# Attention gate: x's high and low parts through one product of four 256-column matmuls, halves added on VectorE

## What is computed

```
q, k, v = x @ Wq, x @ Wk, x @ Wv        # q, k: silu, then a rotation ("rope")
o       = chunked linear attention over q, k, v, with a running state per head
gate    = x @ Wg1 @ Wg2                 # Wg1: 512 x 32, Wg2: 32 x 512
o       = o * sigmoid(gate)
o       = o / sqrt(mean over each head of o*o + eps) * norm_weight
x1      = x + o @ Wo
out     = x1 + down( gelu(n(x1) @ gate_W) * (n(x1) @ up_W) )     # n: layer norm
```

## Time and profile before

| | |
|---|---|
| median of three runs | 1288.82 us (1288.71 to 1288.97) |
| the profiled execution | 1288.75 us, its span 1286.7 us |
| busy share of the span | TensorE 99%, VectorE 71%, ScalarE 37%, GpSimd 34% |
| granted TensorE clock | full speed in every slice of the span |
| attention and passage | the first 300 us or so of the span; `gate1` runs 16 times in them |

### The profile page before, as it was taken

One profiled execution on the slowest core, in us unless ns is written; L12 is line 12 of the kernel. 1 busy time (PEld: TensorE's weight loads), 2 busy tenths in 40 slices (PEclk: granted clock), 3 DMA queues, 4 the chain that ended last, 5 costly groups with the idle time before them and its releaser, 6 DMA issues.

```text
span 1286.7 us, 20699 instructions
## 1 busy us (share of the span) xinstructions
PE 1270.3 (99%) x7376; PEld 1043.5 (81%) x7376; DVE 917.0 (71%) x1594; ACT 475.2 (37%) x799; POOL 435.2 (34%) x360
## 2 busy tenths in 40 slices
PE   9999999998999999999999999999999999999998
PEld 6888888887788888888888888888888888888887
DVE  7878788788867667676767676767767666767665
ACT  5433434434433333333333433333333333333421
POOL 2434455564442322223132324133232324232400
PEclk9999999999999999999999999999999999999999
DMA  9000000000001000010000000001001000000003
GB/s 326 12 2 1 19 17 2 2 1 2 25 25 33 17 33 27 22 33 28 29 24 24 24 24 24 33 16 33 24 24 33 24 33 24 24 24 24 24 13 119
DMA packets 21778, 40.23 MB, mean 31 GB/s; under 512 B 2660, under 2 KB 2916, under 8 KB 21604
## 3 DMA queue, kind: packets, MB, share of 16 engines
q1 hardware_dynamic: 21060, 39.47, 9.4%
q10 hardware_dynamic: 672, 0.13, 0.1%
HBM read 35.40 MB, written 4.19 MB: 31 GB/s over the span
## 4 chain that ended last, share of the span: by engine, by line
PE 93%; DVE 2%; POOL 1%; ACT 1%; issue 1%; POOLq 0%; DVEq 0%; ACTq 0%
PE bank L1351 16%; PE bank L1354 15%; PE bank L1353 15%; PE bank L1197 13%; PE bank L1199 13%; PE bank L1198 13%; PE bank L1211 2%; PE bank L1291 1%; PE bank L1310 1%; PE bank L1300 1%; PE bank L1343 1%; PE bank L1331 1%; PE bank L1258 0%; ACT xg L394 0%; PE bank L1257 0%
## 5 line engine op out<-in xcount | busy, mean ns | idle before, releaser
L883 DVE TENSOR_TENSOR acc<-acc,bank 128x512 f32<-128x512 f32 x248 | 169.3, 683 | 129.4 <-PE bank L1199 129.3
L1197 PE MATMUL bank<-wdh,hh 128*128 128x512 f32 x512 | 199.3, 389 | 0.0
L1199 PE MATMUL bank<-wdh,hl 128*128 128x512 f32 x512 | 199.2, 389 | 0.0
L1198 PE MATMUL bank<-wdl,hh 128*128 128x512 f32 x512 | 199.2, 389 | 0.0
L1351 PE MATMUL bank<-xoh,wgh 128*128 128x512 f32 x448 | 175.9, 393 | 0.6 <-DVE cxa L891 0.6
L1351 PE MATMUL bank<-xoh,wuh 128*128 128x512 f32 x448 | 175.1, 391 | 0.7 <-ACT cxa L482 0.7
L1354 PE MATMUL bank<-xoh,wgl 128*128 128x512 f32 x448 | 174.5, 390 | 0.0
L1354 PE MATMUL bank<-xoh,wul 128*128 128x512 f32 x448 | 174.3, 389 | 0.0
L1353 PE MATMUL bank<-xol,wuh 128*128 128x512 f32 x448 | 174.3, 389 | 0.0
L1353 PE MATMUL bank<-xol,wgh 128*128 128x512 f32 x448 | 174.3, 389 | 0.0
L899 DVE TENSOR_TENSOR hl<-hx,hh 128x512 fp32r<-128x512 f32 x128 | 113.5, 887 | 51.4 <-ACT hh L489 51.0
(11 more groups left out here) (163 smaller groups left out, 2285.7 us busy)
## 6 DMA issues: line engine op xcount, KB each, us to landing
stg<-packed_dram SPq DMA_DIRECT2D x48, 256.0 KB, 2.5
stg<-scales_dram SPq DMA_DIRECT2D x48, 256.0 KB
out_dram<-acc SPq DMA_DIRECT2D x16, 256.0 KB, 2.0
acc<-x_dram SPq DMA_DIRECT2D x3, 1024.0 KB, 15.0
w_in<-wq_dram SPq DMA_DIRECT2D x2, 512.0 KB, 5.2
w_in<-wk_dram SPq DMA_DIRECT2D x2, 512.0 KB, 6.9
w_in<-wv_dram SPq DMA_DIRECT2D x2, 512.0 KB, 8.6
w_in<-wo_dram SPq DMA_DIRECT2D x2, 512.0 KB, 11.2
```

The source lines that it names most:

```text
L883: V.tensor_tensor(row, row, BY[j % 2][:], ALU.add).then_inc(y_add, 1)
L1197: pe.matmul(dst, w_h, x_h, start=start, stop=False)
L1198: pe.matmul(dst, w_h, x_l, start=False, stop=False)
L1199: return pe.matmul(dst, w_l, x_h, start=False, stop=stop)
```

## The change

`gate1` issues one matmul for each of the four channel blocks, over 256 columns: 128 of x's high part and 128 of its low part, side by side, into 256 columns of `BS[3]`. For that the high and low parts of x (and of the output, which tile 1's x borrows) lie in one tile each, `xt` and `ot`; the names `xth`, `xtl`, `oth`, `otl` stay as views of them. The two halves have then to be added. ScalarE copies the first to a new SBUF tile `gs` (`gate_copy`), VectorE adds the second from PSUM into `gs` (`sum_gate`), and the old steps `gate_low` on both engines read `gs` instead of the bank. Two semaphores are new, `g1_sb` and `gate_sum`; TensorE's scores, which reuse the bank, wait for `gate_sum` instead of `g_lo`.

```diff
@@ buffers
-            xth = sb("xth", [P, KT, P], F32R, att)
+            gs = sb("gs", [P, 4, P], F32, att)
-            oth = sb("oth", [P, KT, P], F32R, att)
-            xtl = sb("xtl", [P, KT, P], F32R, att)
+            xt = sb("xt", [P, 2, KT, P], F32R, att)
-            otl = sb("otl", [P, KT, P], F32R, att)
+            ot = sb("ot", [P, 2, KT, P], F32R, att)
+            xth, xtl = xt[:, 0, :, :], xt[:, 1, :, :]
+            oth, otl = ot[:, 0, :, :], ot[:, 1, :, :]
@@ scalar
             def gate_low(t):
+                act.wait_ge(gate_sum, t + 1)
+                act.wait_ge(gate_ps, t)
+                A(g4h[96:128, :], gs[96:128, 1, :], ACT.Copy)
+                A(g4[0:96, :], gs[0:96, 1, :], ACT.Copy).then_inc(g_hi, 1)
+
+            def gate_copy(t):
+
                 act.wait_ge(g1_ps, t + 1)
-                act.wait_ge(gate_ps, t)
-                A(g4h[96:128, :], BS[3][96:128, 0:P], ACT.Copy)
-                A(g4[0:96, :], BS[3][0:96, 0:P], ACT.Copy).then_inc(g_hi, 1)
+                act.wait_ge(gate_sum, t)
+                A(gs[:, 0, :], BS[3][:, 0:P], ACT.Copy).then_inc(g1_sb, 1)
...
                 silu_qk(t + 1)
-                gate_low(t + 1)
+                gate_copy(t + 1)
                 if at_start(b, c):
                     xt_hi_(2)
+                gate_low(t + 1)
                 v_copy(t + 1, (c + 1) % 2)
@@ vector
+            def sum_gate(t):
+
+                dve.wait_ge(g1_sb, t + 1)
+                dve.wait_ge(g_hi, t)
+                V.tensor_tensor(gs[:, 1, :], gs[:, 0, :], BS[3][:, P:2 * P], ALU.add
+                                ).then_inc(gate_sum, 1)
 
             def gate_low(t):
                 dve.wait_ge(g_hi, t + 1)
-                V.tensor_tensor(g4[96:128, :], BS[3][96:128, 0:P], g4h[96:128, :].bitcast(F32),
+                V.tensor_tensor(g4[96:128, :], gs[96:128, 1, :], g4h[96:128, :].bitcast(F32),
                                 ALU.subtract).then_inc(g_lo, 1)
...
                 decayed_q(t)
-                gate_low(t + 1)
+                sum_gate(t + 1)
                 if at_start(b, c):
                     xt_lo_(2)
+                gate_low(t + 1)
                 rope_of(b, c, t + 1, (c + 1) % CHUNKS)
@@ tensor
-                xh, xl = x_of(t)
+                x = ot if isinstance(t, int) and t == 1 else xt
                 for k in range(KT):
-                    g1 = g1s[:, k, :, :].rearrange("p r d -> p (r d)")
-                    pe.matmul(BS[3][:, 0:P], g1, xh[:, k, :], start=(k == 0), stop=False)
-                    ins = pe.matmul(BS[3][:, 0:P], g1, xl[:, k, :], start=False,
-                                    stop=(k == KT - 1))
+                    ins = pe.matmul(BS[3][:, 0:2 * P].rearrange("p (a t) -> p a t", a=2),
+                                    g1s[:, k, :, :].rearrange("p r d -> p (r d)"), x[:, :, k, :],
+                                    start=(k == 0), stop=(k == KT - 1))
...
-                pe.wait_ge(g_lo, t + 2)
+                pe.wait_ge(gate_sum, t + 2)
                 for g in range(KT):
                     scores(g)
```

More of the change, by code:

```diff
@@ L119, in build @@
             xn = sb("xn", [P, 512], F32, att)
-            xth = sb("xth", [P, KT, P], F32R, att)
+            gs = sb("gs", [P, 4, P], F32, att)
             sq = sb("sq", [P, 512], F32, att)
-            oth = sb("oth", [P, KT, P], F32R, att)
+            kd = sb("kd", [P, 512], F32, att)
             wo_h = sb("wo_h", [P, KT, 512], F32R, att)
@@ L128, in build @@
             qa = sb("qa", [P, 2, 512], F32, att)
-            xtl = sb("xtl", [P, KT, P], F32R, att)
-            kd = sb("kd", [P, 512], F32, att)
+            xt = sb("xt", [P, 2, KT, P], F32R, att)
             g1s = sb("g1s", [P, KT, 4, HD], F32R, att)
@@ L212, in build @@
         qk_ps, g1_ps, v_ps, gate_ps = sem("qk_ps"), sem("g1_ps"), sem("v_ps"), sem("gate_ps")
+        g1_sb, gate_sum = sem("g1_sb"), sem("gate_sum")
         g_hi, g_lo = sem("g_hi"), sem("g_lo")
@@ L355, in xt_hi_ @@
                 if t == 1:
-                    A(oth[:], BO[:].rearrange("p (k t) -> p k t", k=KT), ACT.Copy
+                    A(oth, BO[:].rearrange("p (k t) -> p k t", k=KT), ACT.Copy
                       ).then_inc(xt_hi, 1)
@@ L360, in xt_hi_ @@
                     act.wait_ge(v_ps, 1)
-                    A(xth[:], BO[:].rearrange("p (k t) -> p k t", k=KT), ACT.Copy
+                    A(xth, BO[:].rearrange("p (k t) -> p k t", k=KT), ACT.Copy
                       ).then_inc(xt_hi, 1)
@@ L364, in xt_hi_ @@
                 act.wait_ge(v_ps, t)
-                A(xth[:], BV[:].rearrange("p (k t) -> p k t", k=KT), ACT.Copy).then_inc(xt_hi, 1)
+                A(xth, BV[:].rearrange("p (k t) -> p k t", k=KT), ACT.Copy).then_inc(xt_hi, 1)
             def gate_low(t):
+                act.wait_ge(gate_sum, t + 1)
[3 more added lines that the diff above has]
+            def gate_copy(t):
                 act.wait_ge(g1_ps, t + 1)
-                act.wait_ge(gate_ps, t)
-                A(g4h[96:128, :], BS[3][96:128, 0:P], ACT.Copy)
-                A(g4[0:96, :], BS[3][0:96, 0:P], ACT.Copy).then_inc(g_hi, 1)
+                act.wait_ge(gate_sum, t)
+                A(gs[:, 0, :], BS[3][:, 0:P], ACT.Copy).then_inc(g1_sb, 1)
             def silu_qk(t):
@@ L403, in ot_hi_ @@
                 act.wait_ge(wo_ps, t)
-                A(oth[:], BO[:].rearrange("p (k t) -> p k t", k=KT), ACT.Copy).then_inc(ot_hi, 1)
+                A(oth, BO[:].rearrange("p (k t) -> p k t", k=KT), ACT.Copy).then_inc(ot_hi, 1)
             def wide_hi(k, n, dst, piece):
@@ L429, in _ @@
             silu_qk(0)
+            gate_copy(0)
             xt_hi_(1)
@@ L500, in passage @@
                 silu_qk(t)
+                gate_copy(t)
                 gate_low(t)
@@ L672, in xt_lo_ @@
                 if t == 1:
-                    V.tensor_tensor(otl[:], BO[:].rearrange("p (k t) -> p k t", k=KT),
-                                    oth[:].bitcast(F32), ALU.subtract).then_inc(xt_lo, 1)
+                    V.tensor_tensor(otl, BO[:].rearrange("p (k t) -> p k t", k=KT),
+                                    oth.bitcast(F32), ALU.subtract).then_inc(xt_lo, 1)
                     return
                 if t == 2:
-                    V.tensor_tensor(xtl[:], BO[:].rearrange("p (k t) -> p k t", k=KT),
-                                    xth[:].bitcast(F32), ALU.subtract).then_inc(xt_lo, 1)
+                    V.tensor_tensor(xtl, BO[:].rearrange("p (k t) -> p k t", k=KT),
+                                    xth.bitcast(F32), ALU.subtract).then_inc(xt_lo, 1)
                     return
-                V.tensor_tensor(xtl[:], BV[:].rearrange("p (k t) -> p k t", k=KT),
-                                xth[:].bitcast(F32), ALU.subtract).then_inc(xt_lo, 1)
+                V.tensor_tensor(xtl, BV[:].rearrange("p (k t) -> p k t", k=KT),
+                                xth.bitcast(F32), ALU.subtract).then_inc(xt_lo, 1)
+            def sum_gate(t):
[3 more added lines that the diff above has]
+                                ).then_inc(gate_sum, 1)
             def gate_low(t):
                 dve.wait_ge(g_hi, t + 1)
-                V.tensor_tensor(g4[96:128, :], BS[3][96:128, 0:P], g4h[96:128, :].bitcast(F32),
+                V.tensor_tensor(g4[96:128, :], gs[96:128, 1, :], g4h[96:128, :].bitcast(F32),
                                 ALU.subtract).then_inc(g_lo, 1)
@@ L709, in ot_lo_ @@
                 dve.wait_ge(ot_hi, t + 1)
-                V.tensor_tensor(otl[:], BO[:].rearrange("p (k t) -> p k t", k=KT),
-                                oth[:].bitcast(F32), ALU.subtract).then_inc(ot_lo, 1)
+                V.tensor_tensor(otl, BO[:].rearrange("p (k t) -> p k t", k=KT),
+                                oth.bitcast(F32), ALU.subtract).then_inc(ot_lo, 1)
             def add_x1(t):
@@ L787, in _ @@
             dve.wait_ge(s_rot, 16)
+            sum_gate(0)
             rope_of(None, 0, 0, 0)
@@ L925, in passage @@
                 decayed_q(s)
+                sum_gate(t)
                 gate_low(t)
@@ L1469, in passage @@
                 pe.wait_ge(xg_done, s)
-                pe.wait_ge(g_lo, t + 1)
+                pe.wait_ge(gate_sum, t + 1)
                 for g in range(KT):
```

## The result

| | before | changed kernel |
|---|---|---|
| median of 11 runs each, side by side | 1288.97 us (1288.57 to 1290.1) | 1292.48 us (1291.74 to 1294.92) |
| ratio, 95% interval | | 1.0029 [1.0021, 1.0036] |
| profiled execution, its span | 1288.75, 1286.7 | 1292.12, 1290.1 |

The forecast was 1293.0 (1289.5 to 1295.2), slower. It holds. The page's busy shares, against the earlier trace rows: TensorE works 4.8 us less and the kernel takes 3.4 more.

The account below looks back on a forecast made before the run. TensorE is busy 99%, but each tile's last-ending wait is the projection's for VectorE's otl. Ordinary tiles 2.5, tile 8 0.9, tile 10 0.7, tiles 0 and 1 0.1 sum to 4.2: 1288.75 + 4.2 = 1293.0, range 1289.5 to 1295.2.

Parts of the forecast that it names:

- The matmuls: Gate product on TensorE: four of 256 columns at 0.12 each; TensorE reaches everything after it 0.42 sooner.
- rival that 256 columns gain nothing: Gate product: 256 columns cost two of 128; only tile 0 notices, +0.4, 1293.4; 0.66 together with the forecast.
- the hold: VectorE's rope product or subtraction waits behind GpSimd's second rb product, delaying otl; the 0.42 is gone.
- The ordinary tiles' 0.25: Ten tiles (2 to 7, 9, 11 to 13): each loses 0.25 at the projection's wait for otl, +2.5 together.
- copy 135.71 to 135.98 (0.27, as g4h was: Tile 6, first step of the gate's chain: ScalarE's copy of one half, taking 0.27 like g4h before.
- A faster product doesn't start this sooner: Gate's chain, tile 6: its start is unmoved, as ScalarE is at q's and k's activations until 135.68.
- partial hold: Rival: otl comes at 139.4 or earlier; ten tiles cost 0, late ones 1.7; 1290.0, chance 0.16.
- Tiles 0 and 1: First two tiles: tile 0 gains about 0.4, tile 1 loses 0.4 to 0.5; together +0.1.
- about 0.4 gained: Tile 0: nothing stands between; VectorE's delay of 0.3 is covered by its 0.39 wait for the scores.
- by tile 10's working: Tile 1, by tile 10's distances: subtraction issued 46.3, held until 46.8, rope done 48.4; loses 0.4 to 0.5.
- Tiles 8 and 10: Tiles where VectorE comes late: otl delayed by the longer chain, +0.9 in tile 8, +0.7 in tile 10.
- The ends: Ahead of the loop, tile 14 and after: 0 in all; GpSimd's later work 0 to 0.5, taken 0.

Follow-up runs that it names:

- e1: Changed kernel with the four 256-column matmuls but the old gate chain, x's low half left out of the gate: 1285.82 us, ratio 0.9972.
- e11: e5 with the gate product back at eight matmuls of 128 columns: 1290.08 us, ratio 1.0006.
- e8: Changed kernel, but GpSimd starts its two rb products only when VectorE's rope product is done, in all tiles: 1292.81 us, ratio 1.003.
- e2: Changed kernel's longer chain with eight matmuls of 128 columns, four into each half of the bank: 1292.61 us, ratio 1.0022.
- e9: Changed kernel with GpSimd's rb products put behind VectorE's rope product in tiles 1, 8 and 10 alone: 1289.33 us, ratio 1.0.
- e5: e4 plus one wait: GpSimd starts its two rb products only when VectorE's sq is done: 1285.1 us, ratio 0.9968.
- e3: Changed kernel with VectorE's rope product ahead of the g subtraction: 1292.07 us, ratio 1.0021.
- e6: Changed kernel with only a wait added, GpSimd's rb products waiting for VectorE's sq: 1293.87 us, ratio 1.0031.
- e4: Changed kernel with the g subtraction moved behind the masked scores and the x1 add: 1290.34 us, ratio 1.0006.

## Why the prediction was right, and where it was not

- **The matmuls, right.** 0.71 to the second of v, 0.42 a tile. The rival that 256 columns gain nothing is out (e1, e11). The Trainium skill, "TensorE: Matmul & The Clock Gate" (Back-to-back issue gap), would have it gain nothing by its gaps for 128 and 256 columns; its 262 cycles for 256 columns (0.11) are near the measured 0.12, its 134 for 128 (0.06) are half the 0.11 of the earlier trace rows. The prediction took that table without its condition: the section gives it for the isolated matmul, and for a stream in which each matmul has a weight load of its own it gives about 81 ns at 128 columns, which is still below the 0.11 here.
- **That the gain is lost to the hold, right.** e8 shows it as cause in the ordinary tiles, and the rope product's 2.19 lay where it was forecast (2.2).
- **The ordinary tiles' 0.25, wrong by 0.30 each.** The step that failed is the first of the chain, "copy 135.71 to 135.98 (0.27, as g4h was". The copy of 128 rows starts 0.48 after the second `qa`, where g4h, of 32 rows, starts 0.62 after it. It is not the product's speed: e1, with the fast product and the old g4h, has 0.62, and e2, with the slow product and the new copy, 0.48, in every ordinary tile. That "A faster product doesn't start this sooner" stands. With those 0.14 the subtraction was issued 1.77 after `qa` (working: 1.89) and went ahead of GpSimd's second product, which was put off by 0.05 and not by 0.17 (the pair took 2.59 for 2.54). And the rope product's free part with what follows it was about 1.2, not 1.30. So otl began 4.26 after `qa`, forecast 4.5 to 4.6; about half of the difference is the copy's. The rival "partial hold" with its "ten tiles cost 0" describes these tiles.
- **Tiles 0 and 1, wrong by 2.0.** The step that failed is "about 0.4 gained" for tile 0 and "by tile 10's working" for tile 1. The first looked at TensorE alone: tile 0 did give back 0.54, but VectorE left it 0.9 later. The second then took over a distance from another tile without asking which engine gets to the port first in this one. The row that would have told is VectorE's in tile 1 of before: `sq` 0.36 ahead of GpSimd. Only those 0.36 of room stood between this tile and a loss of 2.
- **Tiles 8 and 10, right in kind.** 0.68 and 0.42 for 0.9 and 0.7. In tile 8 `sq` was held again, to 1.72. e9 shows that both are holds: freed of them the tiles gain 0.3.
- **The ends.** The 0.26 lie within the 0 to 0.5 that the text gave for GpSimd's later work; TensorE waited 1.46 for `sq` in the passage, 1.17 before. The 0.60 ahead of the loop were not foreseen: g2s, VectorE's low part of Wg2, came behind GpSimd's sum and took 1.59. Tile 0 did not absorb them: at tile 1's first mark the changed kernel stands at +0.06, e1, which has no such delay, at -0.40.
- **The total.** -0.5 for +2.5, and +2.7 for +0.1, nearly cancel: 3.4 for 4.2. That the gain would be lost rested on the hold and was earned. That the size fits is luck, and only the table by stretch shows it. The clear loss is luck too: with 0.1 instead of 2.7 up to the end of tile 1 the table adds up to some +0.8, which is the "partial hold" rival and not the forecast.

## What to carry to other kernels

Where VectorE and GpSimd both read SBUF, the unit of cost is not the added instruction but the place in which each one stands: look in every tile, the odd ones first, for how far ahead of GpSimd's next instruction VectorE is, and price what happens when that room is gone. A saving on the bound engine moves all of this at once, so a real gain can be paid back in a tile far from the edit (e1's tile 8). When such a race is found, fix its order with a wait that costs nothing or move the subordinate instruction out of it, and see where the pushed work lands (e5 against e8).

## What the runs showed of the hardware

- The hold does not depend on the size of the held instruction. A VectorE step of 16 columns, 0.17 alone, took 1.20 to 1.30 (changed kernel, e1); the subtraction of 32x128 1.26 to 1.37 (e3, e6, tile 0 of the changed kernel). The sum, with one PSUM input, took 0.28 or 0.29 everywhere. That is as the Trainium skill, "GPSIMD Engine Reference" (1. Specifications), would have it, which speaks of VectorE instructions with two SBUF inputs or in a 2-port mode. Two inputs are not needed: in e8 the unpacking step (2.22 for 0.43) and a layer-norm step of 8 columns (1.32) were held with one SBUF input each. Whether they ran in that mode no run shows.
- 0.03 us decide who goes first. In tile 1 of the changed kernel the Newton step came 0.03 after GpSimd's product and lost 1.1. In tile 0 of the kernel before, the last low part of Wo came 0.03 ahead of GpSimd's `kd` and lost nothing, and `kd` took 1.63 (1.29 in the changed kernel).
- After one idle piece of 1.77, TensorE's granted clock fell from 2.4 to 1.2 GHz for some 3.4 us (e6). In e4's tile 1 it fell for as long after a wait of 1.37, and in tile 1 of the changed kernel waits of 1.33 and 1.07, 3 us apart, left it full. In the passage it fell in the profiled executions of e2, e4, e5, e6, e8 and e9, after waits for `sq` of 1.46, 1.16, 1.16, 1.69, 2.55 and 1.19. It stayed full in the seven others, after 1.14 to 1.17 and, in the changed kernel, 1.46. So the length of the wait alone does not tell whether it falls. It takes 1.7 to 3.4 of full speed where it comes. The changed kernel's runs at a mean clock of 1.000 took 1291.74 to 1292.48, and one 1293.4; those at 0.997 to 0.999 took 1292.99 to 1294.92, so most of their spread goes with the clock.
- ScalarE's copy of 128 rows starts 0.12 before the record of a 128-row instruction ahead of it ends; its copies of 32 and 96 rows start 0.01 to 0.04 behind the record ahead. Exchanging one for the other moves a chain by 0.14 with no change of work.
